# Loads of x and stores of the output in DMAs of one slot (512 KB) in place of one unit (1 MB)

## The reference

```python
def layer(x, index, weights):
    w = weights[index]
    return x + jnp.einsum('bct,bcd->bdt', x, w)

x = layer(x, itok_B_0_7, L0_cond_weights)
x = layer(x, itok_B_1_198, L1_cond_weights)
```

## Time and profile before

| | us |
|---|---|
| median of 3 runs | 92.88 |
| lowest, highest | 92.86, 92.94 |
| the profiled execution | 92.97 |
| its span, first to last instruction | 91.2 |
| busy in the span: TensorE matmuls | 79.2 |
| VectorE | 61.8 |
| ScalarE | 58.6 |
| GpSimd | 23.4 |

### The profile page before, as it was taken

The page is one execution under the profiler, slowest core; times in us unless marked ns, Lnnn a source line. Parts: engine busy times, 40 slices in busy tenths (PEclk is TensorE's granted clock), DMA queues, the critical chain, the costliest instruction groups (busy, mean ns, idle before and its releaser), DMA issues.

```text
span 91.2 us, 2427 instructions
## 1 busy us (share of the span) xinstructions
PE 79.2 (87%) x890; PEld 45.6 (50%) x890; DVE 61.8 (68%) x127; ACT 58.6 (64%) x117; POOL 23.4 (26%) x119
## 2 busy tenths in 40 slices
PE   0599979985999999999999999999999999999100
PEld 0488959974454544454454445445545444443000
DVE  1096009996287878787888787888778888788600
ACT  2899806886276776676777576777657676676500
POOL 3400039989999988000000000000000000000000
PEclk9999999999999999999999999999999999999955
DMA  0999999999999999999999999999999999999992
GB/s 12 335 438 422 453 361 420 411 406 415 406 408 408 406 408 413 415 394 417 408 403 415 420 419 420 410 424 415 419 415 419 415 422 422 419 419 404 417 404 104
DMA packets 9181, 35.93 MB, mean 394 GB/s; under 512 B 721, under 2 KB 850, under 8 KB 9042
## 3 DMA queue, kind: packets, MB, share of 16 engines
q1 hardware_dynamic: 8880, 33.56, 91.5%
q0 software_dynamic: 144, 2.10, 5.4%
q10 hardware_dynamic: 146, 0.13, 0.5%
HBM read 19.01 MB, written 16.78 MB: 392 GB/s over the span
## 4 chain that ended last, share of the span: by engine, by line
PE 70%; DMA 12%; DVE 9%; issue 1%; DVEq 1%; ACTq 0%; POOLq 0%
PE psum L229 62%; DMA w_rows<-in_L_cond_weights_dram,cond 10%; DVE w L248 7%; PE psum L210 7%; DMA subjects<-in_itok_B_dram 2%; DVEq L69 1%; DVE xy L270 1%; PE psum L190 1%; DVE m_diag L262 1%; ACTq L319 0%; DVE w_rows L314 0%; POOLq L159 0%; DVEq L254 0%
## 5 line engine op out<-in xcount | busy, mean ns | idle before, releaser
L229 PE MATMUL psum<-xy,m_diag 64*128 64x512 f32 x256 | 57.1, 595 | 0.5 <-DVE m_diag L262 0.5
L270 DVE COPY xy<-psum 64x512 f32<-64x512 f32 x64 | 43.7, 684 | 13.1 <-PE psum L229 12.1
L270 ACT COPY xy<-psum 64x512 f32<-64x512 f32 x64 | 37.2, 581 | 19.8 <-PE psum L229 19.0
L229 PEld LDWEIGHTS psum<-xy,m_diag 64*128 64x128 f32 x256 | 25.2, 187 | 26.7 <-issue 25.4
L167 POOL COPY w0b<-w0t 64x64 f32 x112 | 21.6, 235 | 10.1 <-DMA w_rows<-in_L_cond_weights_dram,cond 8.4
L210 PEld LDWEIGHTS psum<-w,w0b 64*32 64x32 f32 x512 | 5.6, 105 | 6.4 <-issue 3.8
L248 ACT COPY w<-psum 64x256 f32<-64x256 f32 x16 | 5.8, 364 | 4.0 <-PE psum L190 3.0
L180 PE MATMUL psum<-ident,w_rows 128*64 128x128 f32 x54 | 8.1, 326 | 0.0
L262 DVE TENSOR_SCALAR m_diag<-psum,mask 128x256 f32<-128x256 f32 (+1 forms) x18 | 7.2, 448 | 1.1 <-PE psum L210 0.9
L190 PE MATMUL psum<-ident,w_rows 128*64 128x128 f32 x64 | 7.2, 274 | 0.7 <-DVE w_rows L314 0.7
L327 ACT COPY w<-w_rows 128x256 f32<-128x256 f32 x18 | 7.3, 404 | 0.8 <-DMA w_rows<-in_L_cond_weights_dram 0.2
(11 more groups left out here) (8 smaller groups left out, 2.3 us busy)
## 6 DMA issues: line engine op xcount, KB each, us to landing
xy<-in_x_dram SPq DMA_DIRECT2D x15, 1024.0 KB, 18.5
out_dram<-xy SPq DMA_DIRECT2D x15, 1024.0 KB, 14.8
xy<-in_x_dram SPq DMA_DIRECT2D x2, 512.0 KB, 5.9
out_dram<-xy SPq DMA_DIRECT2D x2, 512.0 KB, 4.7
w_rows<-in_L_cond_weights_dram ACTq DMA_DIRECT2D x1, 128.0 KB, 2.5
cond<-in_itok_B_dram SPq DMA_DIRECT2D x1, 0.5 KB, 2.3
subjects<-in_itok_B_dram ACTq DMA_DIRECT2D x1, 0.5 KB
w_rows<-in_L_cond_weights_dram,cond POOLq DMA_INDIRECT x1, 9.3
```

The lines of the kernel that those rows point to most:

```text
L229: last = nc.tensor.matmul(psum[:, 2 * (s % Y_RING) + h, :], m_diag[rows, odd, v % M_RING, j, :], xy[rows, s, j * T:(j + 1) * T], start=j = ...
L270: copy(xy[rows, s, i * T:(i + 1) * T], psum[HALVES[i], 2 * (s % Y_RING) + h, :]).then_inc(done, 1)
```

## The change

All loads of x and all stores go by slots. SP issues slots 0, 1 and 2, waits for the early w0 copies as before, and issues slots 3 to 31. Then it stores slots 0 to 31, each as soon as it is copied. x and output have one semaphore per slot, 64 in place of 32, and TensorE waits for the slot that it works on, not for the unit. Everything else is the same.

```diff
--- before.py
+++ after.py
@@ -110,36 +110,30 @@
         s_y_psum = sem("s_y_psum")
         s_y_v = sem("s_y_v")
         s_y_s = sem("s_y_s")
-        s_x = [sem(f"s_x{n}") for n in range(UNITS)]
-        s_out = [sem(f"s_out{n}") for n in range(UNITS)]
+        s_x = [sem(f"s_x{n}") for n in range(SLOTS)]
+        s_out = [sem(f"s_out{n}") for n in range(SLOTS)]
 
         block = ctx.enter_context(nc.Block())
 
         @block.sync
         def _(sp):
-            def load(s, n):
-                sp.dma_start(xy[:, s:s + n, :], x_view[:, s:s + n, :]).then_inc(s_x[s // 2], 16)
+            def load(s):
+                sp.dma_start(xy[:, s, :], x_view[:, s, :]).then_inc(s_x[s], 16)
 
             sp.dma_start(cond[:, :], cond_dram.rearrange("(b o) -> b o", o=1)).then_inc(s_cond, 16)
-            load(0, 2)
-            load(2, 1)
+            for s in range(3):
+                load(s)
 
             sp.wait_ge(s_w0b_early, EARLY * UNIT)
-            load(3, 1)
-            for v in range(2, UNITS):
-                load(2 * v, 2)
-            def store(s, n):
-
-                sp.wait_ge(s_y_v, 2 * (s + n))
-                sp.wait_ge(s_y_s, 2 * (s + n))
-                sp.dma_start(out_view[:, s:s + n, :], xy[:, s:s + n, :]).then_inc(s_out[s // 2], 16)
-
-            for v in range(UNITS - 1):
-                store(2 * v, 2)
-            store(SLOTS - 2, 1)
-            store(SLOTS - 1, 1)
-            for v in range(UNITS):
-                sp.wait_ge(s_out[v], 32 if v == UNITS - 1 else 16)
+            for s in range(3, SLOTS):
+                load(s)
+            for s in range(SLOTS):
+
+                sp.wait_ge(s_y_v, 2 * (s + 1))
+                sp.wait_ge(s_y_s, 2 * (s + 1))
+                sp.dma_start(out_view[:, s, :], xy[:, s, :]).then_inc(s_out[s], 16)
+            for s in range(SLOTS):
+                sp.wait_ge(s_out[s], 16)
 
         @block.gpsimd
         def _(pool):
@@ -219,7 +213,7 @@
                 pe.wait_ge(s_m_s, 2 * (k + 1))
                 for s in range(2 * first, 2 * (first + n)):
                     v, odd = s // 2, s % 2
-                    pe.wait_ge(s_x[v], 32 if v == 1 else 16)
+                    pe.wait_ge(s_x[s], 16)
                     if s >= Y_RING:
 
                         pe.wait_ge(s_y_v, 2 * (s - Y_RING + 1))
```

## The result

| | kernel before | changed kernel |
|---|---|---|
| median, us | 93.01 (92.86 to 93.45, 6 runs) | 94.32 (93.88 to 94.63, 6 runs) |
| ratio | | 1.0134, 95% interval 1.0111 to 1.0157 |
| profiled execution, us | 92.97 | 94.63 |
| its span, us | 91.2 | 92.8 |

The changed kernel is slower by 1.3%, where 0.24% was forecast. 94.32 lies outside the range of 92.4 to 93.8. The direction was right, the size was off by a factor of more than five.

A forecast was written before the change was run, and what follows sets the result against it. The prediction took the DMA engines as the bound; 0.22 us for small packets, all other terms 0, took the profiled 92.97 us to 93.19, or 93.1 as median (0.24% slower). The range was 92.4 to 93.8 us.

The forecast's parts named there:

- What bounds the kernel: Whole span: the DMA engines bound it from their first packet to about 90 us, so a loss there counts in full.
- The slack of compute: End of the span: the compute path lies 0.7 us below the DMA bound, with 3.9 us per slot on idle engines.
- Packets and their price: All DMA engines: 480 more small completion packets, 30 per engine at 7.2 ns each, add 0.22 us in full.
- No gap between DMAs: DMA queue: a completion costs nothing beyond its packet; taken as 0, with 0.38 us kept for the range.
- no other packet length: Loads: large packets keep their 163.3 ns; taken as 0, with -1.03 and +1.25 us kept as bounds.
- Twice the issues therefore cost nothing.: SP: two store issues take 0.7 us where the DMA engines need 2.5 us per megabyte, so the cost is 0.
- the stretch of slot 3: Early loads: large packets read at 168.5 ns, an instruction fetch among them; for all such loads +1.25 us.
- 0.01 us on TensorE's start, hidden under the DMA bound: Gather of w1 behind slots 0 to 2: same bytes, at most two small packets more per engine, so no visible cost.
- B: Loads up to about 50 us: one-sweep reading makes packets 4.3 ns cheaper, so the kernel gets faster, 92.2 us; chance 0.20.
- D: Every DMA: its fixed 2.6 us comes to light, times 30 is 78 us, some 171 us in all; chance 0.01.
- C: Slots cost more than small packets: a 0.38 us gap gives 93.5, slot 3's packet time in all loads up to 94.3; chance 0.16.
- the sign that would refute it: End of the span: a last store issued later than 86.1 us would mean the compute path moved and the argument is off.

The follow-up runs named there:

- e12: Changed kernel with unit 0 (slots 0 and 1) loaded in one DMA and SP's program cut to 71 instructions by fewer semaphores and waits; 93.40 us, ratio 1.0036.
- e7: Kernel before with only slots 16 to 31 stored singly, 7 DMAs more, 79 SP instructions; 93.13 us, ratio 1.0009.
- e2: Kernel before with units 2 to 15 loaded by slots, 14 DMAs more, first three DMAs and all stores unchanged; 92.99 us, ratio 0.9996.
- e5: Kernel before with 40 idle SP instructions added between the last load and the first store, no DMA changed; 93.50 us, ratio 1.0051.
- e1: Kernel before with unit 0 loaded as two DMAs of 512 KB instead of one; 93.57 us, ratio 1.0080.
- e6: Kernel before with slot 0 loaded alone, then slots 1 and 2 in one 1 MB DMA; 93.87 us, ratio 1.0096.
- e4: Changed kernel with unit 0 (slots 0 and 1) loaded as one 1 MB DMA; 93.88 us, ratio to the kernel before 1.0088.
- e10: e6 with 8 memsets on GpSimd ahead of the gather, so that it is issued 1.3 us later; 96.74 us, ratio to the kernel before 1.0300.
- e11: Kernel before with 8 memsets on GpSimd ahead of the gather, so that it is issued 1.3 us later; 95.91 us, ratio 1.0264.
- e14: Kernel before with one semaphore per slot counted by both VectorE and ScalarE, DMAs unchanged; 93.01 us, ratio 1.0001.

## Why the prediction was wrong

- **What bounds the kernel.** Right: the slowest DMA engine, in the changed kernel too. The slack of compute was put at 0.7 us, from 3.9 us for a slot on idle engines, a figure that came from the first load. That was too long: in the changed kernel 14 of the 16 engines had landed the last store 2.7 us after its issue, which leaves some 1.9 us of slack for stores by slots. A path that was 2.5 us late moved their end by 0.55 us.
- **Packets and their price.** Right in number (480), and right in size as far as it can be seen: 0.22 us forecast, e12 has 0.36% (0.14 to 0.59) for 29 DMAs, e7 0.09% for 7, e2 nothing for 14. No gap between DMAs, no other packet length; both bounds that widened the range were not needed.
- **"Twice the issues therefore cost nothing."** This is the first step that failed. It weighed the time of SP's issues, of which there was plenty, and not the length of SP's program. A row that pointed to it was at hand: the stretch of slot 3 was read with a fetch in it, and the fetch was taken as part of that stretch alone, not as something that a longer program brings more of. In this kernel, which is bound by its DMA engines, an instruction fetch is a cost on the bound resource, on one engine of 16, the one on which the end hangs: 0.51% in e5.
- **The gather: "0.01 us on TensorE's start, hidden under the DMA bound".** The second step that failed. The bytes ahead of the gather were the same, and the mean would have been too; but the gather lands with its slowest engine (in the changed kernel at 13.80 us, the other 15 by 12.99). That engine came 0.4 to 1.1 us later, the warm-up work had been cut to the old landing, in the changed kernel's profile the clock fell to 0.50 for 3.4 us, and the path moved by 2.5 us, more than any slack. And a late engine is late on the bound resource too: in the changed kernel's profile one was 1.2 us behind the others at the first store and never waited for compute again, though part of its delay came after the start and may be due to instruction packets. The first boundary costs 0.45% on top of e12 and 0.80 to 0.96% by itself (e1, e6), with runs that spread more than those of the kernel before.
- **The rivals.** B and D didn't happen. C had the right sign, and its upper end, 94.3, is the measured time, but by luck: it came from a dearer large packet, and that stayed at 163.2 ns; its gap (93.5) didn't come either, the share being 1.020 and 1.022 in the two stretches. The forecast named the sign that would refute it, a last store issued after 86.1 us; it came.

## What to carry to other kernels

Where one DMA engine of 16 ends the kernel, count what lands on single engines, not means: an instruction fetch, an additional boundary, a late start. An edit that puts more DMAs and waits on a queue also lengthens the program of the engine that issues them (here from 65 instructions to 118); count its instructions and look in the trace at which count a fetch comes (here after the 83rd). And where TensorE is kept busy until a transfer lands, that work fits one landing time only: here a gather that landed 1.1 us later cost its delay, and in one profile of the changed kernel the clock behind it as well, 1.3 us more.

## What the runs showed that wasn't expected

- Late in the span an instruction packet of 8 KB on q14, 0.31 to 0.40 us long in the records, came after SP's 80th to 84th instruction in five kernels; in two with 79 in all it came after the last, and in those with 72 or fewer there is none after 36 us. It is taken to be the fetch of SP's program. In e4 one of the 16 DMA engines lands 0.6 us later behind it, the others don't. 40 idle instructions of 0.06 us each, at a place where SP had time to spare, cost 0.5 us (93.50 against 93.00 us, ratio 1.0051).
- With a 512 KB load first in the queue one DMA engine mostly has a packet of 1.1 to 1.5 us near 4.3 us (6 of 7 profiles, e10's among them); with a 1 MB load first the longest was 0.84 us (none of 9 above it). What causes it wasn't found; a collision with GpSimd's DMA_INDIRECT instruction is excluded by e10 and e11.
- The gather's packets weren't interleaved with those of the loads ahead of it: in the kernel before they begin at 6.73 us, when the first engine has done its loads, and between 7.3 and 11.6 us there is no packet of x. So a late engine at the head of the queue can turn into a late gather: in the changed kernel slot 2 lands on 15 engines by 7.92 us and on the last at 8.55, the gather on 15 by 12.99 and on the last at 13.80.
- After the fetch the slowest engine kept losing a little, from 2.48 to 2.83 us behind the first over 13 stores in e4. In the kernel before it lost some too, from 1.66 to 2.02 us over its stores 7 to 13. What does this isn't shown.
- No version beat the kernel before; e14, at 1.0001, is its equal with one wait less per slot.
